# Layer-0 attention on one Trainium2 core: products with V taken for eight key tiles at a time, and the heads' outputs sent through DRAM

## The reference

```python
x_flat = x.reshape(B, C, H * W).transpose(0, 2, 1)
Q, K, V = (split_heads(x_flat @ W + b) for W, b in ((Wq, bq), (Wk, bk), (Wv, bv)))   # 4 heads of 32
attn = jax.nn.softmax(jnp.einsum('bhnd,bhmd->bhnm', Q, K) * scale, axis=-1)
out = jnp.einsum('bhnm,bhmd->bhnd', attn, V)
out = out.transpose(0, 2, 1, 3).reshape(B, H * W, C)
y = (out @ Wo + bo) + x_flat
y = (y - mean(y)) / sqrt(var(y) + 1e-5) * gamma + beta        # over the 128 channels
```

## Time and profile before

| | |
|---|---|
| median of three runs | 6187.24 us (6182.13 to 6188.05) |
| the profiled execution | 6181.0 us, span 6179.2 us |
| TensorE, weight loads | busy 90% and 41% of the span |
| VectorE, ScalarE, GpSimd | busy 79%, 60%, 67% of the span |
| layer 0 | to about 3950 us: TensorE busy without a gap from 100 to 3870 us |
| layer 1 | from about 3970 us to the end: VectorE busy 90% and more |

### The profile page before, as it was taken

How to read it: one execution, slowest core, us unless ns; L and a number is a source line. 1 busy time by engine, 2 the same in 40 slices (tenths; PEclk the granted TensorE clock), 3 DMA queues, 4 the chain that set the end, 5 groups by cost and what they waited for, 6 DMA issues and landing times. The chain is left out here.

```text
span 6179.2 us, 90944 instructions
## 1 busy us (share of the span) xinstructions
PE 5589.3 (90%) x27184; PEld 2550.2 (41%) x27184; DVE 4912.2 (79%) x7188; ACT 3717.1 (60%) x7290; POOL 4118.1 (67%) x3147
## 2 busy tenths in 40 slices
PE   7999999999999999999999999677777777777777
PEld 3444444444444444444444444233333333333332
DVE  7777777777777777777777777299999999999998
ACT  3666666666656666666666666566566656666665
POOL 2677766676766677666677776376676666676776
PEclk9999999999999999999999999899899889988998
DMA  4011011111110110110100000244444444444444
GB/s 132 20 42 40 29 31 34 32 43 30 32 35 25 38 42 29 40 33 23 31 18 12 21 9 21 67 164 144 157 150 143 153 151 148 142 157 149 146 153 144
DMA packets 293852, 465.18 MB, mean 75 GB/s; under 512 B 73680, under 2 KB 97104, under 8 KB 291920
## 3 DMA queue, kind: packets, MB, share of 16 engines
q1 hardware_dynamic: 293360, 459.70, 23.4%
HBM read 381.74 MB, written 76.28 MB: 74 GB/s over the span
## 5 line engine op out<-in xcount | busy, mean ns | idle before, releaser
L560 POOL TENSOR_TENSOR sums<-exps 128x512 f32<-128x512 f32 x2048 | 2617.3, 1299 | 1312.5 <-ACT exps L493 1307.8
L569 DVE TENSOR_REDUCE mpart<-ps 128x1 f32<-128x512 f32 x4096 | 2539.7, 682 | 820.3 <-PE ps L369 820.3
L493 ACT ACTIVATE exps<-ps 128x512 f32<-128x512 f32 x4096 | 2127.9, 603 | 1405.0 <-PE ps L376 1404.6
L1224 POOL TENSOR_TENSOR hc<-hh,c_rep 128x512 f32<-128x512 f32 x1024 | 1422.0, 1393 | 713.1 <-DVE hh L1195 710.7
L369 PE MATMUL ps<-k_st,q_ring 96*128 96x512 f32 x4096 | 1754.1, 429 | 18.4 <-DMA k_st<-qk_split 9.3
L376 PE MATMUL ps<-q_ring,k_st 98*128 98x512 f32 x4096 | 1621.4, 397 | 4.0 <-ACT exps L493 3.6
L1195 DVE TENSOR_TENSOR_SCAN hh<-d_a,carry,ps 128x512 f32<-128x512 f32 x1024 | 1296.0, 1268 | 1.0
L369 PEld LDWEIGHTS ps<-k_st,q_ring 96*128 96x128 f32 x4096 | 774.6, 189 | 1065.0 <-DVE mpart L569 548.7
L387 PE MATMUL ps<-exps,v_ring 128*32 128x512 f32 x8192 | 1090.8, 605 | 0.0
L1016 PE MATMUL ps<-s_u,sel_g 128*128 128x512 f32 x1024 | 665.6, 650 | 232.6 <-DVE hh L1195 230.5
L376 PEld LDWEIGHTS ps<-q_ring,k_st 98*128 98x128 f32 x4096 | 778.3, 190 | 148.2 <-ACT exps L493 17.3
(11 more groups left out here) (106 smaller groups left out, 2906.1 us busy)
## 6 DMA issues: line engine op xcount, KB each, us to landing
d_a<-dt_dram SPq DMA_DIRECT2D x1040, 256.0 KB
qk_split<-hilo SPq DMA_DIRECT2D x128, 256.0 KB, 2.3
q_ring<-qk_split SPq DMA_DIRECT2D x384, 64.0 KB, 2.0
k_st<-qk_split SPq DMA_DIRECT2D x45, 512.0 KB, 7.0
dt_dram<-dt SPq DMA_DIRECT2D x33, 512.0 KB, 2.8
za<-z_ext SPq DMA_DIRECT2D x33, 320.0 KB, 6.1
zp<-z_ext SPq DMA_DIRECT2D x33, 320.0 KB, 8.0
xc<-in_x SPq DMA_DIRECT2D x32, 256.0 KB, 3.1
```

What stands on the lines that cost most here:

```text
L493: nc.scalar.activation(exps[:, u % 4, CH * half:CH * half + CH], a_bank(("exp", n, t)), ACT.Exp, scale=SCALE).then_inc(a_done, 1)
L560: pool.tensor_tensor(sums[:, u % 8, :], exps[:, u % 4, 0:CH], exps[:, u % 4, CH:2 * CH], ALU.add).then_inc(summed, 1)
L569: nc.vector.tensor_reduce(mpart[:, m % 2, t % 4, t // 4:t // 4 + 1], d_bank(("max", m, t)), AX.X, ALU.max).then_inc(d_done, 1)
L1224: pool.tensor_tensor(hc[:, g % NHC, :], hh[:, g % NHH, :], c_rep[:, p, :], ALU.mult).then_inc(hc_ready, 1)
```

## The change

Products with V are issued only after even quads, for two quads at once: behind quad 2 for the quads 0 and 1, behind 4 for 2 and 3, behind 6 for 4 and 5, and behind quad 0 of the next slot for 6 and 7. The sums for the denominators stay where they were, behind the second of the two. So TensorE issues the scores of the quads 1 and 2, 3 and 4, 5 and 6, 7 and 0 as runs of 16 products. `exps` grows to 8 pairs. To make room for it, `heads_out` goes; `read_out` copies into `out_sb` (two chunks), SyncE stores that in DRAM, and in a finishing slot loads the four heads of the chunk back (1 MB, `heads_in`). `spread_den` with its reciprocal moves from v = 4 to 3, `join_heads` and `normalise` from 5 to 4. Nothing else moves.

```diff
+EXPS = 8
...
             if f is not None:
-                if v == 4:
+                if v == 3:
                     add(a, ("den", f))
...
-                if v == 5:
+                if v == 4:
                     add(d, ("join", f))
...
+    out_dram = nc.dram_tensor("out_dram", [2, HEADS, 128, L], F32, kind="Internal").ap()
...
-        exps = sb("exps", [128, 4, 2 * CH])
+        exps = sb("exps", [128, EXPS, 2 * CH])
         sums = sb("sums", [128, 8, CH])
-        heads_out = sb("heads_out", [128, HEADS, L])
+        out_sb = sb("out_sb", [128, 2, CH])
+        heads_in = sb("heads_in", [128, HEADS, CH])
...
+                def store_out(n):
+                    sp.wait_ge(out_read, n + 1)
+                    f = batch_of(n) * NCH + n % NCH
+                    if f >= 2 * NCH:
+                        sp.wait_ge(h_in, 16 * (f - 2 * NCH + 1))
+                    sp.dma_start(out_dram[batch_of(n) % 2, n // NCH % HEADS, :, chunk(n % NCH)], out_sb[:, n % 2, :]
+                                 ).then_inc(out_stored[n % 2], 16)
+
+                def load_heads(f):
+                    if f:
+                        sp.wait_ge(d_ready, d_at["join", f - 1] + 1)
+                    sp.wait_ge(out_stored[f % 2], 16 * (last_slot(f) // 2 + 1))
+                    sp.dma_start(heads_in[:, :, :], out_dram[f // NCH % 2, :, :, chunk(f % NCH)].rearrange("h p l -> p h l")).then_inc(h_in, 16)
...
                     if 0 <= n - 1 < NS:
+                        store_out(n - 1)
                         store_den(n - 1)
+                    if f is not None:
+                        load_heads(f)
                     if 0 <= n + 1 < NS:
                         store_max(n + 1)
...
-                                               exps[:, (2 * v + i // 2) % 4, CH * (i % 2):CH * (i % 2) + CH],
+                                               exps[:, (2 * v + i // 2) % EXPS, CH * (i % 2):CH * (i % 2) + CH],
...
                 def join_heads(f):
-                    pe.wait_ge(out_read, last_slot(f) + 1)
+                    pe.wait_ge(h_in, 16 * f + 16)
...
-                                               heads_out[:, h, chunk(f % NCH)], start=True, stop=True)
+                                               heads_in[:, h, :], start=True, stop=True)
...
-                            if v == 4:
+                            if v == 3:
                                 spread_den(f)
...
                         m, u = (n, v - 1) if v else (n - 1, QUADS - 1)
-                        if 0 <= m < NS:
+                        if 0 <= m < NS and u % 2:
+                            attn_v(m, u - 1)
                             attn_v(m, u)
-                        if f is not None and v == 5:
+                        if f is not None and v == 4:
                             join_heads(f)
                         if 0 <= m < NS and u % 2:
                             sum_exps(m, u)
...
-                    if half == 0 and n * PAIRS + u >= 4:
-                        act.wait_ge(av_done, n * PAIRS + u - 3)
-                        act.wait_ge(summed, n * PAIRS + u - 3)
-                    nc.scalar.activation(exps[:, u % 4, CH * half:CH * half + CH], a_bank(("exp", n, t)), ACT.Exp, scale=SCALE
+                    if half == 0 and n * PAIRS + u >= EXPS:
+                        act.wait_ge(av_done, n * PAIRS + u - EXPS + 1)
+                        act.wait_ge(summed, n * PAIRS + u - EXPS + 1)
+                    nc.scalar.activation(exps[:, u % EXPS, CH * half:CH * half + CH], a_bank(("exp", n, t)), ACT.Exp, scale=SCALE
...
-                    if n // NCH % HEADS == 0 and f >= NCH:
-                        act.wait_ge(d_done, d_at["join", f - NCH] + 1)
-                    nc.scalar.copy(heads_out[:, n // NCH % HEADS, chunk(n % NCH)], ps[:, OUT_BANK, :]).then_inc(out_read, 1)
+                    if n >= 2:
+                        act.wait_ge(out_stored[n % 2], 16 * (n // 2))
+                    nc.scalar.copy(out_sb[:, n % 2, :], ps[:, OUT_BANK, :]).then_inc(out_read, 1)
...
-                        if f is not None and v == 4:
+                        if f is not None and v == 3:
                             reciprocal(f)
...
-                            if v == 5:
+                            if v == 4:
                                 normalise(f)
```

More of the change, by code:

```diff
@@ L224, in layer0 @@
                              "mneg_ready", "mrow_hi")]
-        (made, split_ready, v_stored, recip_ready, squared, rstd_ready, scale_ready, z_ready, z_stored, f_in) = [
+        (made, split_ready, v_stored, recip_ready, squared, rstd_ready, scale_ready, z_ready, z_stored, f_in, h_in) = [
             sem(s) for s in ("made", "split_ready", "v_stored", "recip_ready", "squared", "rstd_ready", "scale_ready", "z_ready",
-                             "z_stored", "f_in")]
+                             "z_stored", "f_in", "h_in")]
         q_in = [sem(f"q_in{i}") for i in range(4)]
         k_piece = [sem(f"k_piece{i}") for i in range(NCH)]
-        k_in, v_in, x_in, split_stored, mrow_stored, den_stored = [
-            [sem(f"{s}{i}") for i in range(2)] for s in ("k_in", "v_in", "x_in", "split_stored", "mrow_stored", "den_stored")]
+        k_in, v_in, x_in, split_stored, mrow_stored, den_stored, out_stored = [
+            [sem(f"{s}{i}") for i in range(2)] for s in ("k_in", "v_in", "x_in", "split_stored", "mrow_stored", "den_stored",
+                                                         "out_stored")]
         MAX_BANK, EXP_BANK, OUT_BANK, DEN_BANK = 0, 3, 6, 7
@@ L497, in read_out @@
                     act.wait_ge(av_done, n * PAIRS + PAIRS)
-                    f = batch_of(n) * NCH + n % NCH
-                    if n // NCH % HEADS == 0 and f >= NCH:
-                        act.wait_ge(d_done, d_at["join", f - NCH] + 1)
-                    nc.scalar.copy(heads_out[:, n // NCH % HEADS, chunk(n % NCH)], ps[:, OUT_BANK, :]).then_inc(out_read, 1)
+                    if n >= 2:
+                        act.wait_ge(out_stored[n % 2], 16 * (n // 2))
+                    nc.scalar.copy(out_sb[:, n % 2, :], ps[:, OUT_BANK, :]).then_inc(out_read, 1)
                 def add_bias(p, i):
@@ L559, in _ @@
                             pool.wait_ge(sum_used, n * PAIRS + u - 7)
-                        pool.tensor_tensor(sums[:, u % 8, :], exps[:, u % 4, 0:CH], exps[:, u % 4, CH:2 * CH], ALU.add).then_inc(summed, 1)
+                        pool.tensor_tensor(sums[:, u % 8, :], exps[:, u % EXPS, 0:CH], exps[:, u % EXPS, CH:2 * CH], ALU.add).then_inc(summed, 1)
             @block.vector
```

## The result

The changed kernel takes 6295.78 us (median of 4 runs, 6290.69 to 6300.54), beside 6187.65 (4 runs, 6182.13 to 6198.22) for the kernel before: ratio 1.0173, with an interval of 1.0155 to 1.019. The profiled execution took 6300.54, its span 6297.7. The prediction was 6290, from 6215 to 6350.

The account below looks back on a forecast made before the run. Layer 0 was taken as bound by TensorE at the pace of its starts; 73 x 0.66 = 48, 24 x 1.38 = 33, 31 x 0.67 = 21 and tail 4 gave +106 on 6181.0: 6287, stated as 6290 us, range 6215 to 6350.

Parts of the forecast that it names:

- The ring in a run of 16: Quads 3-4, 5-6, 7-0 of plain slots: three banks make max tiles wait for reductions, 0.37 in all; run 7.06, +0.06.
- Quads 1 and 2: Plain slots: late copy of denominators and two small VectorE operations in mid-run delay the last max tile; 7.86 against 7.38, +0.48.
- What two groups with V save when together: TensorE, each pair of quads: a second group costs 0.88 instead of 1.19 alone, saving 0.31, or 159 us overall.
- What VectorE cost before the change: Old kernel, quads 1 and 2: TensorE waited only 0.15 for the fourth max tile.
- Projection slots: 24 slots: low-part subtraction between reductions gives +0.81 in quads 3-4 and 5-6; -0.30 and +0.06 elsewhere; +1.38 per slot.
- Finishing slots: 31 slots that finish a chunk: ScalarE's work in mid-run delays the exponentials; +0.67 per slot, 21 us in all.
- The last two slots: End of layer 0, without max tiles: not costed apart, taken as finishing slots.
- The way through DRAM: SyncE's stores and 1 MB loads of heads: nothing in the slots, +4 us (0 to 8) behind the last.
- the sum of +106: Whole kernel: 48 for plain slots, 33 with projection, 21 finishing and 4 for the tail, in us.
- That the banks come free in time: Rival on the max-tile ring: reductions 0.50 apart or closer, the 0.31 kept, 6032 us; chance 0.12.
- The clock: Rival: TensorE's pauses lower its granted clock to 0.90 in layer 0, total to some 6700 us; chance 0.03.
- The heads: Rival: the 1 MB load takes 20 us, each join waits some 6, total 6475 us; chance 0.03.

Follow-up runs that it names:

- Experiment 1: Changed kernel with each max-tile reduction over its first 256 columns instead of 512, which changes the computation: 6059.95 us, ratio 0.9785.
- Experiment 4: Changed kernel with the transposed maxima moved from v = 1 to 2 and low-part subtractions from v = 3, 5 to 4, 6: 6232.34 us, ratio 1.0069.
- Experiment 2: Kernel before the change, with each max-tile reduction over 256 columns instead of 512: 6130.28 us, ratio 0.9898.
- experiment 3: Changed kernel with the old order and four pairs in `exps` restored, leaving only the way through DRAM: 6194.92 us, ratio 1.0012.
- experiment 7: Changed kernel with six V groups per slot, behind tiles 6, 11, 16, 22, 27, 32, and small VectorE operations at run ends: 6147.02 us, ratio 0.9947.
- experiment 5: Changed kernel with the max tiles' PSUM ring cut from three banks to two: 6735.74 us, ratio 1.0891.

## Why the prediction was right, step by step

- **The ring in a run of 16.** Predicted: tiles 5, 6 and 7 wait, 0.60 apart, last exp product at 4.00, run of 7.06. Found: the same three tiles (counted from 0; the sixth to the eighth above), the last exp product 4.01 behind the first (164.28 to 168.29), 7.05. Experiment 1 took the cause away and the waits were gone from the plain runs, and 236 us of the time with them.
- **Quads 1 and 2.** Predicted 7.86, found 7.83 (156.45 to 164.28). Experiment 4 confirms how much of it are the two small operations: 0.27.
- **What two groups with V save when together.** Predicted 0.31, measured 0.33 where VectorE doesn't hold the ring.
- **What VectorE cost before the change.** Mis-sized: I put the wait of quads 1 and 2 at 0.15. Experiment 2 shows 0.29 per plain slot, 0.49 with a projection and 0.69 when finishing. It was to be read from the prediction's own numbers, 7.38 for that pair and 7.00 for the others: 0.38, of which the transposed maxima's product is 0.13 (6.78 and 6.65 in experiment 1). It doesn't touch the sum, which went by whole pairs, but it is why experiment 2 missed.
- **Projection slots.** Predicted +1.38, found +1.50: 8.99, 7.81, 8.83 and 7.05 for the four pairs of quads. The two slots in which a chunk's end and a projection meet (+2.16) were not costed apart.
- **Finishing slots.** Predicted +0.67, found +0.43 in most. Every pair was put 0.03 to 0.12 too high (found 8.54, 9.22, 8.10, 7.83). In quads 3-4 the last exp product comes 5.22 behind the first, where I had 5.40. ScalarE's work in mid-run delays it by 0.34 (it starts at 1030.22, 0.57 and not 0.235 behind the product ahead of it), where I had 0.65; TensorE without it would be at 4.88, where I had 4.75.
- **The last two slots.** Not costed: +7.4, ScalarE's work in mid-run and the clock. By luck it made up for the finishing slots (21 expected, 13 found), so that the sum of +106 came out better (+107.9) than its parts.
- **The way through DRAM.** Predicted nothing in the slots and +4 behind them; found +4.1 on the trace and +4.4 (0.6 to 15 by the ratio's interval) in experiment 3.
- **The rivals.** That the banks come free in time fell with the pitch of 0.60. The clock fell only in the last two slots (for 7 and 3 us) and behind them, where it is low before the change too (0.50 from 4042 to 4089, and from 3945 to 3980 before). That it hardly counted holds for three banks: with two the clock fell in 13 finishing slots. The heads kept no slot waiting: the join behind the last slot is the only one of 32 with a wait for its DMA.

The Trainium skill's rule in "TensorEngine Tiling", section PSUM Bottleneck, that with faster TensorE work the emptying of PSUM may become the limit, was the one to follow; experiments 1 and 2 agree, with 236 us between long and short reductions in the changed order and 60 in the old one. Experiments 4 and 7 show it with the work unchanged.

## What to carry to other kernels

A group of other products between the products that fill a PSUM ring is not only a cost: it is when the reader catches up. Before taking it out, compare the pitch of filling with the pitch of emptying (0.47 and 0.60 here) and count how many tiles the banks cover; the longest run without a wait, here five tiles for three banks, is where the groups belong (experiment 7). Whatever else the reading engine does goes to the end of a run, since in its middle it is paid in full.

## What the runs showed that I had not expected

**VectorE's operations between SBUF tiles become longer when they start earlier in one of GpSimd's sums.** The subtraction of the low parts takes 0.82 in the kernel before and 1.47 in experiment 2. On DVE's timeline of experiment 2:

```profile
127.67 1.47 DVE L599 TENSOR_TENSOR hilo<-full,hilo 128x512 fp32r<-128x512 f32 x1
...
134.65 1.47 DVE L599 TENSOR_TENSOR hilo<-full,hilo 128x512 fp32r<-128x512 f32 x1
```

on POOL's:

```profile
127.32 5.76 POOL L560 TENSOR_TENSOR sums<-exps 128x512 f32<-128x512 f32 x4 [2.13 <-ACT exps L493]
134.30 5.57 POOL L560 TENSOR_TENSOR sums<-exps 128x512 f32<-128x512 f32 x4 [1.22 <-ACT exps L493]
```

and on POOL's in the kernel before:

```profile
134.70 5.76 POOL L560 TENSOR_TENSOR sums<-exps 128x512 f32<-128x512 f32 x4 [2.14 <-ACT exps L493]
```

It started 0.35 after the sum in both cases of experiment 2, and 1.01 after it before. It ended 1.82, 1.82 and 1.83 after the sum's start: the end hangs on GpSimd's sum, not on its own start. So faster reductions bought nothing at this place, since they brought the subtraction forward to where it waits. The same is seen in the changed kernel, where `scaled` (L654) takes 1.60 in the median of 32 and took 0.83 before: in 26 slots it starts 0.23 after one of GpSimd's sums, 1.00 before, and in both kernels all 28 that overlap a sum end 0.55 after that sum's end. The last four of the 32 have no sum beside them in either kernel, and take 0.69. In experiment 1 it starts ahead of the sum beside it (by 0.43 in most slots) and takes 0.68 or 0.69 all 32 times; there it is the sum that takes longer, 1.40 instead of 1.28. The Trainium skill, "SBUF — State Buffer", section Who interferes with whom, says that a VectorE operation with two inputs in SBUF contends with a GpSimd operation that reads SBUF, and that of two operations that want the shared pair of ports the one issued first blocks the other; the rows agree. No run here took GpSimd's sums away, but the same operation with and without a sum beside it is in the traces, 0.69 and 0.82 to 1.77.

**Pauses of the same length sometimes lower the clock and sometimes don't.** In the last two slots of the changed kernel it fell in quads 3-4, behind pauses of 0.22 and 0.32. The quads 1-2 just ahead of them have pauses of 0.22, 0.32 and 0.64 (3972.78 to 3976.38), and the clock stayed at 1.00. The order of the change isn't needed for it: in the last slot of experiment 3, with the old order, the clock was 0.50 from 3915.9 to 3919.1 behind pauses of 0.22 and 0.27, and in the last but one of experiment 2 from 3828.0 to 3831.2. In experiment 5 it fell in some finishing slots and not in others with the same program. What sets them apart wasn't tried.
